# Delta mixer: query, key and value of both flights in one set of fp32r products, half a pair ahead

## What is computed

```python
q, k, v, z = split(hidden @ w_qkvz.T)                     # per key head: 128, 128, 256, 256
q, k, v = split(silu(causal_depthwise_conv(concat(q, k, v), conv_w)))    # 4 taps
g = -exp(A_log) * softplus(a + dt_bias); beta = sigmoid(b)
q, k = q * rsqrt(sum(q*q) + 1e-6), k * rsqrt(sum(k*k) + 1e-6)
for t:                                                    # per head, 128 x 128 state S
    S = S * exp(g[t]);  delta = (v[t] - k[t] @ S) * beta[t]
    S = S + outer(k[t], delta);  o[t] = (q[t] * scale) @ S
out = rmsnorm(o * silu(z)) * norm_w @ w_out.T
```

## Time and profile before

| | us |
|---|---|
| median of 3 runs (3974.97 to 3980.59) | 3978.43 |
| the profiled execution | 3979.25 |
| its span | 3977.5 |
| TensorE busy in it | 3679.3 (93%) |
| DVE busy | 2155.0 (54%) |
| ACT busy | 1703.8 (43%) |
| POOL busy | 500.7 (13%) |

### The profile page before, as it was taken

One profiled execution on the slowest core, in us unless ns is written; L12 is line 12 of the kernel. 1 busy time (PEld: TensorE's weight loads), 2 busy tenths in 40 slices (PEclk: granted clock), 3 DMA queues, 4 the chain that ended last, 5 costly groups with the idle time before them and its releaser, 6 DMA issues. The chain is left out here.

```text
span 3977.5 us, 57381 instructions
## 1 busy us (share of the span) xinstructions
PE 3679.3 (93%) x19830; PEld 2912.3 (73%) x19830; DVE 2155.0 (54%) x4759; ACT 1703.8 (43%) x4092; POOL 500.7 (13%) x342
## 2 busy tenths in 40 slices
PE   5997999996899999999999999999999997799998
PEld 2434787883778778788788787787787885687787
DVE  6773555553564554554655645645545554455454
ACT  3342223221554554555555545545545543322321
POOL 1123003000011111111110111101101100301200
PEclk8998999998999999999999999999999999899999
DMA  4003103012000000000000000000000000212110
GB/s 155 22 21 117 43 32 126 33 36 89 17 1 0 23 1 1 23 1 1 23 1 1 23 1 1 23 1 1 23 1 1 17 11 27 102 42 85 64 53 32
DMA packets 56731, 126.25 MB, mean 32 GB/s; under 512 B 2864, under 2 KB 4016, under 8 KB 55472
## 3 DMA queue, kind: packets, MB, share of 16 engines
q1 hardware_dynamic: 56496, 123.26, 8.7%
HBM read 98.09 MB, written 25.17 MB: 31 GB/s over the span
## 5 line engine op out<-in xcount | busy, mean ns | idle before, releaser
L1734 PE MATMUL banks<-b_x_cur,b_w_cur 128*128 128x256 f32 x2048 | 526.4, 386 | 7.9 <-ACT b_w_cur L1196 7.1
L1555 DVE COPY_PREDICATED b_Tt<-b_new_part,banks 128x256 f32<-128x256 uint8 x320 | 157.8, 493 | 672.6 <-PE banks L1806 672.6
L895 PE MATMUL banks<-f_x_hi,f_w_hi 128*128 128x512 f32 x1024 | 408.5, 399 | 38.8 <-ACT f_silu L764 20.3
L895 PE MATMUL banks<-f_x_lo,f_w_hi 128*128 128x512 f32 x1024 | 406.6, 397 | 0.0
L895 PE MATMUL banks<-f_x_hi,f_w_lo 128*128 128x512 f32 x1024 | 406.4, 397 | 0.0
L1734 PEld LDWEIGHTS banks<-b_x_cur,b_w_cur 128*128 128x128 f32 x2048 | 356.3, 191 | 48.5 <-issue 8.4
L1292 ACT COPY b_em<-banks 128x256 f32<-128x256 f32 x320 | 120.5, 377 | 547.5 <-PE banks L1792 547.5
L1792 PE MATMUL banks<-b_T,b_At 128*128 128x128 f32 x2560 | 345.5, 278 | 0.5 <-ACT b_T L1283 0.5
L1806 PEld LDWEIGHTS banks<-b_Tt,b_em 128*128 128x128 f32 x2560 | 332.0, 191 | 17.6 <-ACT b_em L1292 1.1
L1471 DVE SCALAR_TENSOR_TENSOR b_conv<-b_raw,b_taps,b_conv 128x256 f32<-128x256 f32 x768 | 335.0, 501 | 9.6 <-ACT b_conv L1233 9.6
L1806 PE MATMUL banks<-b_Tt,b_em 128*128 128x128 f32 x2560 | 338.0, 275 | 0.9 <-ACT b_em L1292 0.6
(11 more groups left out here) (256 smaller groups left out, 6623.2 us busy)
## 6 DMA issues: line engine op xcount, KB each, us to landing
f_x_tok<-rows SPq DMA_DIRECT2D x16, 1024.0 KB, 7.3
b_w_load<-in_b_qkvz SPq DMA_DIRECT2D x8, 1536.0 KB, 7.2
f_stage<-in_ffn_gate SPq DMA_DIRECT2D x8, 1024.0 KB, 6.5
f_stage<-in_ffn_up SPq DMA_DIRECT2D x8, 1024.0 KB, 7.5
f_stage<-in_ffn_down SPq DMA_DIRECT2D x8, 1024.0 KB, 4.9
f_x_res<-rows SPq DMA_DIRECT2D x8, 1024.0 KB, 5.6
f_part<-f_x_res SPq DMA_DIRECT2D x8, 1024.0 KB, 4.3
f_x_res<-f_part SPq DMA_DIRECT2D x8, 1024.0 KB, 5.6
```

Source lines behind the costliest of these rows:

```text
L895: mm = pe.matmul(bank, w[:, b, kind, cols], x[:, k, :], start=(k == 0 and i == 0), stop=(k == KD - 1 and i == 2))
L1555: dve.copy_predicated(half(f.Tt, i + 1, 1), new_part[:, i, :].rearrange("p (a n) -> p a n", n=LEVELS[i + 1]), half(f.right, i + 1, 1)).the ...
L1734: mm = pe.matmul(bank[i][:, 2 * part:2 * part + 2, :], w_cur[:, k, col:col + P], f.x_cur[:, k, :, :], start=(k == 0), stop=(k == KD - 1))
```

## The change

The two flights' query, key and value are projected together, 512 columns at a time (2 sequences x 2 chunks). Each operand is split in an fp32r high part and the rest, and a product becomes three: high x high, high weights x low x, low weights x high x (`project`). ACT makes the high weights (4 x 512 columns, `high_weights`), in the level i = 2 of the pair before `turn`; POOL makes the low weights, and per pair the high and low x (`split_x`) and a plain copy of x for z (`plain_x`). z stays plain fp32, with weights of its own (`w_z`, a DMA of its own), flight A in bank 0, flight B in bank 1. Query and key of pair m + 2 are projected in the tail of pair m, value and z of pair m + 1 in the start and the levels. Raw copies are one feature each; taps are 512 columns wide, 4 first ones on ACT and 12 on DVE a pair, all between or just behind the levels. Some buffers are shared: `g_hi` and `g_lo` by the flights, `d` with `At`, `junk` with `d_end`, `o` with `T`. The inner loop runs over one pair; the pair before `turn` stands apart.

```diff
-        w_load = sb("w_load", [P, KD, QK])
-        w_cur = sb("w_cur", [P, KD, QK])
+        w_load = sb("w_load", [P, KD, 4 * P])
+        w_hi, w_lo = (sb(n, [P, KD, 4 * P], F32R) for n in ("w_hi", "w_lo"))
+        w_z = sb("w_z", [P, KD, 2 * P])
+        x_hi, x_lo = (sb(n, [P, KD, BATCH, 2 * P], F32R) for n in ("x_hi", "x_lo"))
+        x_cur = sb("x_cur", [P, KD, BATCH, 2 * P])
...
-        raw = sb("raw", [P, 4, BATCH, HALO + P])
+        raw = sb("raw", [P, 4, BATCH, HALO + 2 * P])
+        conv = sb("conv", [P, 4, BATCH, 2 * P])
+        g_hi, g_lo = (sb(n, [P, U, P], F32R) for n in ("g_hi", "g_lo"))
...
-                self.d, self.d_end, self.At, self.Pt = (buf(n) for n in ("d", "d_end", "At", "Pt"))
+                self.d_end, self.At, self.Pt = (buf(n) for n in ("d_end", "At", "Pt"))
+                self.d, self.junk = self.At, self.d_end
...
+                self.X, self.qs, self.o = self.em, self.T, self.T
...
-                    sp.wait_ge(s["wcp"], h)
-                sp.dma_start(w_load[:, :, :], w["b_qkvz"].rearrange("(k p) n -> p k n", p=P)
-                             [:, :, h * QK:(h + 1) * QK]).then_inc(s["w"], 16)
+                    sp.wait_ge(s["wlo"], KD * h)
+                qkvz = w["b_qkvz"].rearrange("(k p) n -> p k n", p=P)
+                sp.dma_start(w_load[:, :, :], qkvz[:, :, h * QK:h * QK + 4 * P]).then_inc(s["w"], 16)
+                if h > 0:
+                    sp.wait_ge(s["pz"], 2 * h * PAIRS)
+                sp.dma_start(w_z[:, :, :], qkvz[:, :, h * QK + 4 * P:(h + 1) * QK]).then_inc(s["wz"], 16)
...
+            def split_x(q, c):
+                pool.wait_ge(s["pj"], 4 * q)
                 pool.sem_inc(s["gate"], 1)
-                pool.tensor_copy(f.x_cur[:, :, :, :], xT[:, :, :, bass.ds(c * P, P)]).then_inc(s["xcur"], 1)
-
+                pool.tensor_copy(x_hi[:, :, :, :], xT[:, :, :, bass.ds(c * P, 2 * P)]).then_inc(s["xhi"], 1)
+                pool.wait_ge(s["xhi"], q + 1)
+                for k in range(KD):
+                    pool.sem_inc(s["gate"], 1)
+                    pool.tensor_tensor(x_lo[:, k, :, :], xT[:, k, :, bass.ds(c * P, 2 * P)], x_hi[:, k, :, :],
+                                       ALU.subtract).then_inc(s["xlo"], 1)
+
+            def plain_x(q, c):
+                pool.wait_ge(s["pz"], 2 * q)
+                pool.sem_inc(s["gate"], 1)
+                pool.tensor_copy(x_cur[:, :, :, :], xT[:, :, :, bass.ds(c * P, 2 * P)]).then_inc(s["xcur"], 1)
+
+            def low_weights(h):
+                pool.wait_ge(s["whi"], h + 1)
+                for k in range(KD):
+                    pool.tensor_tensor(w_lo[:, k, :], w_load[:, k, :], w_hi[:, k, :], ALU.subtract).then_inc(s["wlo"], 1)
...
-                if not last:
-                    chunk_of_x(B, 1 if turn else c + 3, 2 * m + 2)
                 if ahead:
-                    chunk_of_x(A, 0 if over else 2 if turn else c + 4, 2 * m + 3)
+                    c2 = 0 if over else 2 if turn else c + 4
+                    split_x(m + 2, c2)
+                    if over:
+                        low_weights(h + 1)
+                    plain_x(m + 2, c2)
...
+            split_x(0, 0)
+            low_weights(0)
+            plain_x(0, 0)
+            split_x(1, 2)
+            plain_x(1, 2)
...
+            def high_weights(h):
                 act.wait_ge(s["w"], 16 * (h + 1))
-                act.wait_ge(s["pz"], h * CHUNKS)
-                act.copy(w_cur[:, :, :], w_load[:, :, :]).then_inc(s["wcp"], 1)
+                act.wait_ge(s["pj"], 4 * h * PAIRS)
+                act.copy(w_hi[:, :, :], w_load[:, :, :]).then_inc(s["whi"], 1)
...
+            def copy_raw(i, q):
+                act.wait_ge(s["pj"], 4 * q + i + 1)
+                act.wait_ge(s["halo"], q + 1)
+                act.copy(raw[:, i, :, HALO:], flat(bank[i % 2]).rearrange("p (b t) -> p b t", b=BATCH)
+                         ).then_inc(s["raw"], 1)
+
+            def first_tap(i, q):
+                act.wait_ge(s["raw"], 4 * q + i + 1)
+                act.wait_ge(s["mask"], LV)
+                for f in flights:
+                    act.wait_ge(f.s["silu"], q)
+                act.activation(conv[:, i, :, :], raw[:, i, :, 0:2 * P], ACT.Copy, scale=taps[:, i, 0:1]
+                               ).then_inc(s["tap"], 1)
+
+            def copy_z(f, q):
+                act.wait_ge(s["pz"], 2 * q + f.i + 1)
+                act.wait_ge(f.s["zact"], q)
+                act.copy(f.z_raw[:, :, :], bank[f.i][:, :, :]).then_inc(s["zraw"], 1)
...
                 if not last:
-                    copy_qk_or_v(0, 2 * m + 2)
+                    copy_raw(2, m + 1)
                 level(A, m, 0)
+                if not last:
+                    first_tap(0, m + 1)
                 values(B, m)
                 turned(A, m, 1)
                 level(A, m, 1)
+                if not last:
+                    first_tap(1, m + 1)
                 turned(B, m, 0)
                 level(B, m, 0)
                 for i in range(2, LV):
                     turned(A, m, i)
                     if i == 2 and not last:
-                        copy_qk_or_v(1, 2 * m + 2)
+                        copy_raw(3, m + 1)
+                        if over:
+                            high_weights(h + 1)
                     level(A, m, i)
                     turned(B, m, i - 1)
-                    if i == 3 and not last:
-                        first_taps(A, m + 1, 2 * m + 2)
+                    if 2 <= i <= 3 and not last:
+                        first_tap(i, m + 1)
                     level(B, m, i - 1)
                     if i == 4 and not last:
-                        copy_z(A, m + 1, 2 * m + 2)
+                        copy_z(A, m + 1)
                 from_state(A, m)
                 turned(B, m, LV - 1)
+                if not last:
+                    copy_z(B, m + 1)
                 level(B, m, LV - 1)
                 solved(A, m)
                 if not last:
                     silu_qkv(A, m + 1)
-                    copy_qk_or_v(0, 2 * m + 3)
+                    silu_z(A, m + 1)
                 mean_square(A, m)
...
                 from_state(B, m)
-                if not last:
-                    copy_qk_or_v(1, 2 * m + 3)
+                if ahead:
+                    copy_raw(0, m + 2)
                 solved(B, m)
                 output_T(A, m)
-                if not last:
-                    first_taps(B, m + 1, 2 * m + 3)
-                    silu_z(A, m + 1)
                 mean_square(B, m)
-                if not last:
-                    copy_z(B, m + 1, 2 * m + 3)
-
+                if ahead:
+                    copy_raw(1, m + 2)
...
+            def convolve(i, tap, q):
+                if tap == 1:
+                    dve.wait_ge(s["tap"], 4 * q + i + 1)
+                else:
+                    dve.wait_ge(s_conv[i], 3 * q + tap - 1)
+                dve.scalar_tensor_tensor(conv[:, i, :, :], raw[:, i, :, tap:tap + 2 * P], taps[:, i, tap:tap + 1],
+                                         conv[:, i, :, :], ALU.mult, ALU.add).then_inc(s_conv[i], 1)
...
+                steps = {(2, 0): [(0, 1)], (2, 1): [(1, 1), (0, 2)], (3, 0): [(1, 2)], (3, 1): [(0, 3), (2, 1)],
+                         (4, 0): [(1, 3)], (4, 1): [(2, 2), (3, 1)], (5, 0): [(2, 3)], (5, 1): [(3, 2)]}
                 for i in range(2, LV):
-                    level(A, m, i)
-                    if i > 2 and not last:
-                        convolve(A, 2 * m + 2, i - 2)
-                    level(B, m, i - 1)
+                    for f in flights:
+                        level(f, m, i - f.i)
+                        if not last:
+                            for feature, tap in steps[i, f.i]:
+                                convolve(feature, tap, m + 1)
                 right_side(A, m)
                 if not last:
-                    halo(2 * m + 3)
+                    convolve(3, 3, m + 1)
                 to_the_end(A, m)
                 level(B, m, LV - 1)
...
+                if over:
+                    head_taps(h + 1)
+                elif ahead:
+                    halo(m + 2)
...
                 if not last:
                     log_decays(A, m + 1, h + 1 if turn else h, 0 if turn else c + 2)
-                    convolve(B, 2 * m + 3, 1)
                 mean_square(B, m)
                 add_up(A, m, c)
                 normalised(B, m)
...
-                    convolve(B, 2 * m + 3, 2)
-                    convolve(B, 2 * m + 3, 3)
...
+            def project(i, q, k, h=None):
+                if k == 0:
+                    if i < 2:
+                        pe.wait_ge(s["zraw"], 2 * q - 1 + i if not isinstance(q, int) or q > 0 else 0)
+                        pe.wait_ge(s["xhi"], q + 1)
+                    else:
+                        pe.wait_ge(s["raw"], 4 * q + i - 1)
+                if i < 2:
+                    pe.wait_ge(s["xlo"], KD * q + k + 1)
```

(56 more changed lines are left out.)

217 lines of the change are left out of this document (93 added, 124 removed).

## The result

The changed kernel takes 3957.43 us (median of 5 runs, 3956.74 to 3961.96) against 3979.66 for the kernel before, run beside it: ratio 0.9948, interval 0.9934 to 0.9961. That is 22 us, half of the 45 that were forecast, and inside the range. The profiled execution has a span of 3957.9 us against 3977.5.

The account below looks back on a forecast made before the run. TensorE seemed to set the time, with start and tail as chains through ACT, DVE and POOL. Pairs 31, turns 14, last pairs 2, less 2 for jumps, gave 45 us: 3979 to 3934 us, range 3887 to 3972.

Parts of the forecast that it names:

- (6): First and last pairs, loop's jump: 0 us ahead of the loop, 2 us gained at the end, 2 us lost to jumps.
- the way into the loop: Ahead of the loop: POOL's eight subtractions against cheaper projections and fewer convolution steps, taken as zero, bounds -5 and +5 us.
- (2): Tail of a pair: shorter pieces gain 0.2 us; the later solve of A is absorbed before B's product with the state.
- the second last pair: Loses its eight tail pieces: 1.0 us gained, plus 1 for ACT and DVE, 2 us in all.
- (1): TensorE's projections: 48 fp32r products, 11.1 us instead of 13.8, so 2.7 us less work per pair.
- the rival that all comes back: All 2.7 us of TensorE time per pair are gained: 100 us in total, 3879 us; chance 0.15.
- (3): Start of a pair: `b_Tt` of A comes 0.5 us earlier, `b_Tt` of B 0.8 us; 0.8 us gained per pair.
- (4): Turn of a head: ACT's weight copy leaves the pair's start; seven turns gain 2.0 us each, 14 us, bounds 0 and 16.
- (5): POOL's added work per pair, 9 us instead of 2.1, falls where nothing else is asked of it: free.
- The rival that its subtractions hold the predicated copies: In the levels, POOL's subtractions stall DVE's predicated copies: 2.5 us per pair, 79 us, 4013 us; chance 0.14, of it 0.10 slower.
- Holes of up to 1.4 us should not do this: TensorE's clock: holes of this length should not lower the granted clock, as the 2.08 us hole in the last pair did.

Follow-up runs that it names:

- The experiment with the high part alone: Changed kernel with only the high x high product kept for query, key and value, 32 of 48 products per pair dropped: 3964.30 us, ratio 0.9962.
- the filled jump: Changed kernel with TensorE repeating 16 transposes in the pair after each outer jump: loop 2238.0 us instead of 2241.6, one profiled execution.
- both attempts to free it: GpSimd's parts put before its mask copies, on the changed kernel: 3957.31 us; low x made by VectorE, on the kernel with everything together: 3894.75 us.
- Both fixes: On the changed kernel, ScalarE's second bank copy moved to the next pair's start: 3943.09 us; loops over heads written out on all engines: 3936.43 us.

## Why the prediction was right in its parts and wrong in its sum

The step that failed most is the jump's in (6): 2 us charged, 9.7 more lost. Next come the way into the loop (0 charged, some 6 us missing with the first pair, part of it scatter), the tail of (2) (0.2 us a pair forecast, 0 measured, so 6 us, of which the better start gave back some) and the second last pair (3 us).

**(1) TensorE's work: right.** 48 products, 0.23 to 0.24 us apart, make the 11.1 us of the sum, and most of the saving is hidden. The experiment with the high part alone shows it from the other side, and refutes the rival that all comes back.

**(2) The tail: the term of 0.2 us was wrong, it measured 0.** The step of 512 columns takes 0.74 us where 0.70 was taken (median of the loop 0.745), which is no error to speak of. What failed is the sentence that the later solve of A "is absorbed before B's product with the state". It isn't: the tail is a chain from the solve of A to the end. The solve came 0.26 us later (0.3 forecast), and cost what the shorter pieces gave. Moved out of the way the same step gave 0.57 us a pair, so the change paid for its place in `steps` with some 16 us.

**(3) The start: right.** 0.8 us forecast at B's transposes, 0.90 measured; at A's, where 0.5 was forecast, 0.81, with the hole of 1 us and the stretched product, and the masked decay's share shown by taking it away.

**(4) The turn: right.** 3.08 us gained on the pair that ends a head, 0.49 on the one ahead of it, against 3.26 and 0.7.

**(5) GpSimd: right in the levels, wrong ahead of the loop.** The rival that its subtractions hold the predicated copies falls: the one that stands wholly beside a subtraction is as long as without it (0.74 and 0.72 us), and the levels are as long as before. "Free" was said of the loop only, but the same subtractions and VectorE meet in the prologue, which (6) took as zero. VectorE's timeline there, between the first step of the softplus chain and the reciprocal, beside GpSimd's; then the kernel before:

```profile
997.74 1.36 DVE L1477 TENSOR_SCALAR b_qkv<-b_qkv 128x256 f32<-128x256 f32 x1
...
1004.39 1.99 DVE L1485 TENSOR_TENSOR b_qkv<-b_qkv 128x256 f32<-128x256 f32 x1
```

```profile
998.91 5.29 POOL L1157 TENSOR_TENSOR b_w_lo<-b_w_load,b_w_hi 128x512 fp32r<-128x512 f32 x4
```

```profile
996.21 0.29 DVE L1436 TENSOR_SCALAR b_qkv<-b_qkv 128x256 f32<-128x256 f32 x1
...
998.46 0.43 DVE L1444 TENSOR_TENSOR b_qkv<-b_qkv 128x256 f32<-128x256 f32 x1
```

The chain takes 14.6 us instead of 8.6. In this profile the first decays come 2.5 us later than before. The two profiles of the old prologue have 79.5 and 83.1 us, seven of the new one 84.9 to 89.4, so 1.8 us is the least of it and 6.5 the difference of the means: just outside the bounds of 5 around the zero of (6). Another 3.2 us are missing in the first pair, behind whose holes of 1.33 and 1.87 us the clock falls (0.61 in one stretch). In the profile of the filled jump the same pair kept its clock and took 70.2 us instead of 71.8, so half of that is the clock. That the held-up chain alone causes the later decays was not shown: both attempts to free it brought no time, and in both the clock behind the longer wait took back what was won.

**(6) The jump: the term that failed most, 2 us charged and 9.7 more lost.** I had counted the jump as a fixed extra on a pair that otherwise gains its 1.0 us. In fact it is a date: ScalarE's first instruction comes 3.3 to 3.5 us after the decays of A (3.0 to 3.3 before) whatever TensorE and VectorE have gained, so the gain of the start is void there, and the longer hole costs the clock in three of six. Both fixes show it. The second last pair failed by the clock and by the step of (2): 2 us were to be gained by leaving its work out, and behind the two holes of 1.2 us the clock ate it. With the step moved, the first of them is 0.55 us and the pair takes 69.23 us, 3.1 less than before, where 3 was forecast; but the last pair then pays 2.5.

**The clock.** "Holes of up to 1.4 us should not do this" is refuted by the second last pair (1.21 us, with 0.77 ahead of it), and behind the jump the change made holes of 2 us where 1.4 had been the longest. The length of one hole does not decide by itself: in the kernel with the masked decay on VectorE a fall stands behind a hole of 2.32 us and none behind one of 2.37.

## What to carry to other kernels

Before counting what a cheaper product gives, take a pair of the loop that lacks the work and read its length: it shows how much of the time is waits, and leaving work out can cost more than it gives when the holes lower TensorE's clock. A loop's jump is a date for each engine, so put it ahead of a wait that the engine has anyway, or write the loop out. When a step is placed "in a free slot" of VectorE, ask who waits for the instruction behind it, and which GpSimd instruction with SBUF operands runs beside it.
